# An expert layer on one core: three input buffers, layer norm two batches ahead, probabilities scaled in the transposing matmul

## The chip, the cores and the metric

One core of one Trainium2 chip runs the whole program. The metric is the device time in microseconds (us), the median of a few runs; lower is better. A core has five engines with queues of their own: TensorE (PE), VectorE (DVE), ScalarE (ACT), GpSimd (POOL) and SyncE (SP), which here issues the DMAs.

## What is computed

The reference chains four transformer-like layers over x (16 batches of 256 tokens, 128 wide), with a context of 1601 tokens. The change touches only the second, an expert layer with a cross attention in front. Cut to what matters, in the order of the kernel (weights folded so that the context is used as it comes):

```python
n   = layer_norm(x, eps=1e-5) * gamma + beta          # 256 x 128
q   = n @ Wq
s   = (q @ Wk.T) @ ctx.T / sqrt(128)                  # 256 x 1601
p   = softmax(s)                                      # exp, sum, division by the sum
ev  = (p @ ctx) @ Wv                                  # 256 x 128
f   = concat(n, ev, anchor)                           # anchor: a vector for each batch
r   = softmax(f @ router_W + router_b)                # 3 experts
e_i = gelu_like(f @ e_w1[i] + e_b1[i]) @ e_w2[i] + e_b2[i]
g   = sigmoid(silu(f @ gate_w1 + gate_b1) @ gate_w2 + gate_b2)
out = x + g * ((sum_i r_i * e_i) @ out_w + out_b)
```

All is fp32. The attention layers before and after it are phases of their own.

## The kernel before

`layers` (L1596) runs four parts one after the other, each with its own buffers, semaphores and block: `modulation`, an attention phase (names pa_...), `expert_layer` (L1105, names moe_...), a second attention phase (pb_...). A part starts when the one before it has ended on all engines.

In `expert_layer` a batch has a front F (layer norm, q, transposes of the context, scores, softmax, transposes of the probabilities, pooling of the context, ev) and a back B (router, three experts, gate, output). Steps of the front: ln, xt (xn transposed), q, qk, c0 to c3 (context tiles transposed, four in a step, the last step one), s0 and s1 (scores and softmax of each half of 128 queries), p00 to p03 and p10 to p13 (probabilities of half 0 and 1 transposed, 13 tiles of 128 keys each), pc (26 matmul records: probabilities times context), ev. Steps of the back: r (router), h0, h1, h2 (first expert matmuls), g1, e0, e1 (second expert matmuls and weighting for each half), g2, rt, o.

`walk` (L1214) calls these steps on each engine in one order written out by SCHED. First the whole front of batch 0; then body b runs the back of batch b interleaved with the front of batch b+1, in this order: F ln, B r, F xt, F q, B h0, F qk, F c0, B h1, F c1, F c2, B h2, F c3, F s0, B g1, F s1, F p00, B e0, F p01, F p02, B e1, F p03, F p10, B g2, F p11, F p12, B rt, F p13, F pc, B o, F ev. The last body has only the back. Every engine takes its own share of each step in that order, so a waiting instruction holds up all behind it on its engine.

Who does what: VectorE has ln (L1289 to L1303, 21 instructions, each waiting for the one before it), the copies of c1 and c3, in s0 and s1 the row maxima (L1317), their negation (L1319, L1321), the sum and its reciprocal rec (L1323, L1327), the copies of p01, p03, p11, p13 (`move_probs`, L1241 and L1243), the small router softmax, the products of h and g1 (L1363, L1360), the weighting in e0 and e1 (L1380, L1382). ScalarE has the copies of xt, q, qk, c0, c2, pc, ev, p00, p02, p10, p12, the exp of the scores (L1437) and the tanh of experts and gate. GpSimd has two things: the division of the probabilities by their sum, prn = pr * rec over 128x1601 (L1483), and the final addition xo = y + xin (L1491). TensorE transposes prn in L1549.

Front results go through two PSUM banks in turn: step i of the front writes bank i % 2 and waits until step i-2 is copied out (`bank_free`, L1206). So p02 waits for the copy of p00, p03 for that of p01, and so on.

SP's queue (L1247): `load_x` fetches x, the modulation columns acols and the router row rrow of a batch into one of two buffers each, and waits until the batch two before it is summed (x_sum), because the final addition reads xin; `load_c` fetches the context tile cin (single buffer, 800 KB) and waits for pc of the batch before it; `store` writes xo. Order: load_x(0), load_c(0), load_x(1), load_c(1), store(0), then load_x(k), load_c(k), store(k-1).

Of the kernel before, what the change touches and what calls it, by code (L numbers as in the profile page):

```python
# [17 lines left out]
ALU = mybir.AluOpType  # L18
# [3 lines left out]
P = 128  # L22
B = 16
# [1081 lines left out]
def expert_layer(nc, w, x_src, x_dst, ctx_d, cols_d, rows_d, ident_d, nb):  # L1105
# [20 lines left out]
    with Semaphores(nc) as sems, ExitStack() as ctx:  # L1126
# [17 lines left out]
        xin = [sb(f"xin{i}", [P, QT, D]) for i in range(2)]  # L1144
# [13 lines left out]
        prn = [sb(f"prn{i}", [P, KEYS]) for i in range(QT)]  # L1158
# [15 lines left out]
        x_in, c_in = [sem("x_in0"), sem("x_in1")], sem("c_in")  # L1174
# [17 lines left out]
        X_LOADS = 3 * 16  # L1192
# [21 lines left out]
        def walk(eng, front, back):  # L1214
            def body(b, w, has_next):
                for kind, k in SCHED:
                    if kind == "F" and has_next:
                        front(k, b + 1, 1 - w)
                    elif kind == "B":
                        back(k, b, w)  # L1220
# [26 lines left out]
        def _(sp):  # L1247
# [3 lines left out]
            def load_x(n, w):  # L1251
# [22 lines left out]
            if nb > 2:  # L1274
                for i in range((nb - 2) // 2):
                    for k, w in ((2, 0), (3, 1)):
                        load_x(i * 2 + k, w)
                        load_c(i * 2 + k)
                        store(i * 2 + k - 1)
            store(nb - 1)  # L1280
# [3 lines left out]
        def _(dve):  # L1284
# [4 lines left out]
            def front(k, n, w):  # L1289
                if k == "ln":  # L1290
                    dve.wait_ge(x_in[w], (n - w) * (X_LOADS // 2) + X_LOADS)
                    wait(dve, x_ln, n * QT)
                    link = Chain(dve, ln_dve, n * LN_PER)
                    for t in range(QT):
                        link(dve.bn_stats(st[:, t, :], xin[w][:, t, :]))
# [6 lines left out]
                    for t in range(QT):  # L1302
                        dve.tensor_scalar(xn[:, t, :], xin[w][:, t, :], ag[:, t, 0:1], rs_y[:, t:t + 1], ALU.subtract, ALU.mult).then_inc(x_ln, 1)  # L1303
# [7 lines left out]
                elif k in ("s0", "s1"):  # L1311
# [86 lines left out]
        def _(act):  # L1398
# [5 lines left out]
            def front(k, n, w):  # L1404
# [26 lines left out]
                elif k in ("s0", "s1"):  # L1431
# [3 lines left out]
                    wait(act, s_norm, after(n - 1, QT, qt))  # L1435
# [6 lines left out]
            def back(k, d, w):  # L1442
# [219 lines left out]
```

## Time and profile before

| | |
|---|---|
| time, median of 3 runs | 6419.06 us (6411.44 to 6420.05) |
| profiled execution, own time | 6427.87 us |
| its span | 6426.1 us |
| mean granted TensorE clock | 0.899 |
| PE busy in the span | 5152.7 us (80%) |
| DVE, ACT, POOL busy | 64%, 58%, 27% |
| expert layer in the span | about 2080 to 3042 us |

The profile is of one execution. Times are in us from the start of its span. PE is TensorE's matmuls, PEld its weight loads, which run beside them. "L1549" is a line of the kernel. An entry such as `moe_bank_f<-moe_ident,moe_prn` is output, then inputs, by the program's names, without buffer numbers. `x8` is a count of records; an fp32 matmul is recorded twice, a transpose once. In brackets stands how long the engine had been idle before the first of them, and what ended that. The granted clock is a share of 2.4 GHz: 1.00 is 2.4 GHz, 0.50 is 1.2 GHz.

### The profile page before, as it was taken

What the parts mean: (1) busy time and instruction counts of PE and PEld (TensorE: products, weight loads), DVE (VectorE), ACT (ScalarE), POOL (GpSimd) and SP (SyncE); (2) the same over time, 40 slices, a digit from 0 to 9 for tenths busy, and PEclk for the clock granted to TensorE, in tenths of its full rate; (3) what the DMA queues carried; (4) which work ended last, traced back from release to release, by engine and by line L of the source; (5) the groups of instructions that cost most, each with busy time, mean ns of one, the idle gap of its engine ahead of it and who ended that gap; (6) DMA issues with size and microseconds to landing.
All of it is one profiled execution on the core that took longest, in us unless ns stands there. A gap on an engine that the chain in (4) does not pass through costs nothing.

```text
span 6426.1 us, 123739 instructions
## 1 busy us (share of the span) xinstructions
PE 5152.7 (80%) x48177; PEld 2416.8 (38%) x48177; DVE 4087.9 (64%) x8759; ACT 3696.1 (58%) x5043; POOL 1731.6 (27%) x2614
## 2 busy tenths in 40 slices
PE   3688888888886776776598888888888888888887
PEld 1233333333332555555233333333333333333333
DVE  3476767777763333333577777676777777677674
ACT  1266667676665222222266666666677776666665
POOL 1433343433321111111223232323221322322311
PEclk9699999999988778887589999999999999999998
DMA  1121111111110000000211111111121111111110
GB/s 39 56 57 46 54 40 48 55 45 52 39 41 22 19 14 21 21 16 20 58 38 55 55 47 54 49 49 54 38 66 55 48 47 37 49 49 37 51 39 6
DMA packets 362967, 271.14 MB, mean 42 GB/s; under 512 B 47905, under 2 KB 324991, under 8 KB 362385
## 3 DMA queue, kind: packets, MB, share of 16 engines
q1 hardware_dynamic: 362384, 263.23, 14.4%
q8 instruction: 384, 6.29, 0.4%
q14 instruction: 199, 1.62, 0.1%
HBM read 86.96 MB, written 12.78 MB: 16 GB/s over the span
## 4 chain that ended last, share of the span: by engine, by line
PE 30%; DVE 10%; ACT 6%; issue 4%; POOL 3%; SPq 0%; DMA 0%; ACTq 0%; POOLq 0%
PE pb_obank L896 11%; DVE pb_c_maxs L584 8%; PE pb_dbank L909 6%; PE pb_aunit L871 5%; ACT pb_probs L653 4%; PE pb_aunit L950 2%; PE pb_aunit L943 2%; PE pb_aunit L935 1%; POOL pb_c_cin L770 1%; PE pb_dbank L957 1%; DVE pb_z_maxs L584 1%; PE pb_aunit L983 1%; PE pb_aunit L977 1%; ACT pb_c_srct L686 0%; POOL pb_c_cs_y L766 0%
## 5 line engine op out<-in xcount | busy, mean ns | idle before, releaser
L584 DVE TENSOR_REDUCE pb_c_maxs<-pb_dbank 128x1 f32<-128x512 f32 (+1 forms) x3584 | 2046.7, 627 | 871.1 <-PE pb_dbank L909 862.1
L653 ACT ACTIVATE pb_probs<-pb_aunit 128x1024 f32<-128x1024 f32 (+1 forms) x1792 | 1753.0, 1024 | 598.6 <-PE pb_aunit L871 540.5
L584 DVE TENSOR_REDUCE pa_c_maxs<-pa_dbank 128x1 f32<-128x512 f32 (+1 forms) x1792 | 1025.5, 627 | 470.3 <-PE pa_dbank L909 468.1
L653 ACT ACTIVATE pa_probs<-pa_aunit 128x1024 f32<-128x1024 f32 (+1 forms) x960 | 936.6, 1024 | 296.8 <-PE pa_aunit L871 264.6
L896 PE MATMUL pb_obank<-pb_probs,pb_c_vaug 128*9 128x256 f32 x13312 | 991.3, 398 | 8.5 <-ACT pb_probs L653 7.5
L909 PE MATMUL pb_dbank<-pb_c_kst,pb_c_qst 48*128 48x512 bf16 (+1 forms) x4096 | 854.9, 354 | 115.6 <-DVE pb_c_maxs L584 91.9
L871 PE MATMUL pb_aunit<-pb_c_qst,pb_c_kst 50*128 50x256 bf16 x6144 | 616.6, 284 | 99.2 <-ACT pb_probs L653 55.3
L909 PEld LDWEIGHTS pb_dbank<-pb_c_kst,pb_c_qst 48*128 48x128 bf16 x4096 | 248.1, 95 | 703.7 <-DVE pb_c_maxs L584 454.9
L896 PE MATMUL pa_obank<-pa_probs,pa_c_vaug 128*9 128x256 f32 x6656 | 489.5, 392 | 5.6 <-ACT pa_probs L653 5.3
L909 PE MATMUL pa_dbank<-pa_c_kst,pa_c_qst 48*128 48x512 bf16 (+1 forms) x2048 | 420.4, 354 | 53.4 <-DVE pa_c_maxs L584 46.2
L871 PEld LDWEIGHTS pb_aunit<-pb_c_qst,pb_c_kst 50*128 50x128 bf16 x6144 | 257.9, 97 | 373.4 <-ACT pb_probs L653 121.1
L896 PEld LDWEIGHTS pb_obank<-pb_probs,pb_c_vaug 128*9 128x9 f32 x13312 | 251.3, 91 | 385.2 <-issue 228.9
L871 PE MATMUL pa_aunit<-pa_c_qst,pa_c_kst 50*128 50x256 bf16 x3072 | 303.5, 280 | 56.1 <-ACT pa_probs L653 31.2
L1483 POOL TENSOR_SCALAR moe_prn<-moe_pr,moe_rec 128x1601 f32<-128x1601 f32 x32 | 138.7, 4336 | 558.4 <-DVE moe_rec L1327 558.4
L909 PEld LDWEIGHTS pa_dbank<-pa_c_kst,pa_c_qst 48*128 48x128 bf16 x2048 | 120.6, 95 | 338.4 <-DVE pa_c_maxs L584 203.2
L584 DVE TENSOR_REDUCE pa_z_maxs<-pa_dbank 128x2 f32<-128x512 f32 x256 | 163.6, 684 | 118.8 <-PE pa_dbank L909 118.8
L784 POOL TENSOR_TENSOR pb_c_kf<-pb_c_kf,pb_c_ksp 128x1024 f32<-128x1024 f32 x64 | 114.4, 1787 | 318.0 <-ACT pb_c_ksp L697 318.0
L871 PEld LDWEIGHTS pa_aunit<-pa_c_qst,pa_c_kst 50*128 50x128 bf16 x3072 | 123.4, 96 | 200.4 <-ACT pa_probs L653 68.8
L896 PEld LDWEIGHTS pa_obank<-pa_probs,pa_c_vaug 128*9 128x9 f32 x6656 | 123.5, 90 | 188.4 <-issue 107.7
L1437 ACT ACTIVATE moe_pr<-moe_bank_s,moe_nm 128x400 f32<-128x400 f32 (+1 forms) x128 | 74.4, 594 | 169.2 <-DVE moe_nm L1321 169.2
L584 DVE TENSOR_REDUCE pb_z_maxs<-pb_dbank 128x2 f32<-128x512 f32 x256 | 164.0, 683 | 0.8 <-PE pb_dbank L909 0.8
L751 POOL TENSOR_SCALAR pb_c_rs_v<-pb_c_agg 128x2 f32<-128x2 f32 x32 | 7.9, 246 | 547.2 <-DVE pb_c_agg L598 547.1
(446 smaller groups left out, 7070.9 us busy)
## 6 DMA issues: line engine op xcount, KB each, us to landing
pb_c_kst<-pb_c_ksp SPq DMA_DIRECT2D x384, 200.1 KB
pa_c_kst<-pa_c_ksp SPq DMA_DIRECT2D x192, 200.1 KB
pb_c_cin<-in_ctx SPq DMA_DIRECT2D x32, 768.0 KB
pa_c_cin<-in_ctx SPq DMA_DIRECT2D x16, 768.0 KB
moe_cin<-in_ctx SPq DMA_DIRECT2D x16, 768.0 KB
pb_c_qst<-pb_c_qsp SPq DMA_DIRECT2D x384, 32.0 KB
pa_z_qst<-pa_z_qsp SPq DMA_DIRECT2D x192, 32.0 KB
pa_z_kst<-pa_z_ksp SPq DMA_DIRECT2D x192, 32.0 KB
```

The costliest lines, as they stand in the source:

```text
L584: dve.tensor_reduce(dst, dbank[N % RING_D][:, 0:cnt * width].rearrange("p (s c) -> p s c", s=cnt), AX.X, ALU.max).then_inc(d_free, 1)
L653: act.activation(probs[u % RING_P][0:rows].rearrange("p a i q -> p (a i q)"), src[0:rows, :], ACT.Exp, scale=HD ** -0.5).then_inc(a_free, 1)
L770: pool.tensor_scalar(s.cin[0:rows, t, :], s.cin[0:rows, t, :], s.cs_m[0:rows, t:t + 1], s.cs_y[0:rows, t:t + 1], ALU.add, ALU.mult).then_i ...
L784: pool.tensor_tensor(s.kf[:, part], s.kf[:, part], s.ksp[:, 0, part], ALU.subtract).then_inc(s.k_r, 1)
L871: ins = pe.matmul(dst[:, par * 512 + h * NQ:par * 512 + (h + 1) * NQ], s.kst[b2][lo:lo + K_ROWS + 2, pair, t * P:(t + 1) * P], s.qst[b2][l ...
L896: ins = pe.matmul(obank[32 * h4:32 * h4 + HD + 1, half * NQ:(half + 1) * NQ], s.vaug[i % 2][0:rows, t, 4 * q + h4, :], src, start=(t == 0) ...
L909: ins = pe.matmul(dbank[nd[tok, s.key, i, par] % RING_D][:, col:col + width], s.qst[b2][lo:lo + K_ROWS, p, qt * P:(qt + 1) * P], s.kst[b2] ...
L935: ins = pe.transpose(dst[:, (t - t0) * P:(t - t0) * P + rows], s.cin[0:rows, t, :], ident[0:rows, 0:rows])
L943: ins = pe.matmul(dst[:, at - t0 * P:at - t0 * P + width], w.wkp[:], src[:, at:at + width], start=True, stop=True)
L950: ins = pe.matmul(dst[0:rows, (t - t0) * P:(t - t0 + 1) * P], (s.srct if s.has_ctx else s.xmt)[:, t * P:t * P + rows], w.wv[:], start=True ...
L1437: act.activation(pr[qt][:, at:at + width], sbank[c][:, 0:width], ACT.Exp, bias=nm[:, qt:qt + 1], scale=D ** -0.5, accum_out=sums[:, qt, c: ...
L1483: pool.tensor_scalar(prn[qt][:], pr[qt][:], rec[:, qt:qt + 1], None, ALU.mult).then_inc(s_norm, 1)
```

## The change

- x has three buffers (xin[n % 3]) and a semaphore for each; it is loaded two batches ahead. acols and rrow keep two buffers, have semaphores of their own (cols_in) and are loaded by `load_cols`. r (VectorE) and h0 to g1 (ScalarE) wait for cols_in, ln waits for x alone.
- `walk`: ln leaves its place at the head of the body. ln of batch 1 comes after the front of batch 0; in body b, ln of batch b+2 comes behind entry 15 of the order, that is behind F p00 and ahead of B e0. For VectorE that is behind s1 and ahead of e0, since p00 is not its step.
- GpSimd no longer divides. VectorE makes a diagonal matrix diag = ident * rec (128x128) for each half, at the end of s0 and s1, and TensorE replaces each transpose of a prn tile by an fp32 matmul of the undivided tile pr with diag, which transposes and scales at once.
- ScalarE's exp waits for the last p step of the batch before instead of for the division.
- SP's order: load_x(0), load_c(0), load_x(1), load_cols(0), then for each n: load_x(n+2), load_cols(n+1), load_c(n+1), store(n).

```diff
-        xin = [sb(f"xin{i}", [P, QT, D]) for i in range(2)]
+        xin = [sb(f"xin{i}", [P, QT, D]) for i in range(3)]
...
-        prn = [sb(f"prn{i}", [P, KEYS]) for i in range(QT)]
+        diag = [sb(f"diag{i}", [P, P]) for i in range(QT)]
...
         def walk(eng, front, back):
...
             for kind, k in SCHED:
                 if kind == "F":
                     front(k, 0, 0)
-            body(0, 0, True)
-            if nb > 2:
-                for i in range((nb - 2) // 2):
-                    body(i * 2 + 1, 1, True)
-                    body(i * 2 + 2, 0, True)
-            body(nb - 1, 1, False)
+            front("ln", 1, 1)
+            for b in range(nb):
+                for at, (kind, k) in enumerate(SCHED):
+                    if kind == "F" and k != "ln" and b + 1 < nb:
+                        front(k, b + 1, (b + 1) % 2)
+                    elif kind == "B":
+                        back(k, b, b % 2)
+                    if at == len(SCHED) // 2 and b + 2 < nb:
+                        front("ln", b + 2, b % 2)
...
+            def load_x(n):
+                if n < nb:
+                    wait(sp, x_sum, n - 2)
+                    sp.dma_start(xin[n % 3][:], x_src[n].rearrange("(t p) d -> p t d", p=P)).then_inc(x_in[n % 3], 16)
+
+            def load_cols(n):
+                w = n % 2
                 wait(sp, x_sum, n - 1)
-                sp.dma_start(xin[w][:], x_src[n].rearrange("(t p) d -> p t d", p=P)).then_inc(x_in[w], 16)
-                sp.dma_start(acols[w][:], cols_d[n]).then_inc(x_in[w], 16)
-                sp.dma_start(rrow[w][:], rows_d[n][ROUTER_ROW:ROUTER_ROW + 1, 0:EXPERTS].to_broadcast([P, EXPERTS])).then_inc(x_in[w], 16)
+                sp.dma_start(acols[w][:], cols_d[n]).then_inc(cols_in[w], 16)
+                sp.dma_start(rrow[w][:], rows_d[n][ROUTER_ROW:ROUTER_ROW + 1, 0:EXPERTS].to_broadcast([P, EXPERTS])).then_inc(cols_in[w], 16)
...
-            load_x(0, 0)
+            load_x(0)
             load_c(0)
-            load_x(1, 1)
-            load_c(1)
-            store(0)
...
+            load_x(1)
+            load_cols(0)
+            for n in range(nb):
+                load_x(n + 2)
+                if n + 1 < nb:
+                    load_cols(n + 1)
+                    load_c(n + 1)
+                store(n)
...
-                    wait(dve, s_norm, after(n - 1, QT, qt))
                     dve.reciprocal(rec[:, qt:qt + 1], tot[:, qt:qt + 1]).then_inc(s_rec, 1)
+                    dve.wait_ge(s_rec, after(n, QT, qt))
+                    wait(dve, f_full, after(n - 1, UF, F_AT[f"p{qt}{len(TG) - 1}"]))
+                    dve.tensor_scalar(diag[qt][:], ident[:], rec[:, qt:qt + 1], None, ALU.mult).then_inc(s_norm, 1)
...
-                if k in ("s0", "s1"):
-                    qt = int(k[1])
-                    pool.wait_ge(s_rec, after(n, QT, qt))
-
-                    wait_apart(pool, f_full, after(n - 1, UF, F_AT[f"p{qt}{len(TG) - 1}"]), (ready, 1))
-                    pool.tensor_scalar(prn[qt][:], pr[qt][:], rec[:, qt:qt + 1], None, ALU.mult).then_inc(s_norm, 1)
+                return
...
-                        ins = pe.transpose(dst[0:rows, (t - t0) * P:(t - t0 + 1) * P], prn[qt][:, t * P:t * P + rows], ident[:])
+                        ins = pe.matmul(dst[0:rows, (t - t0) * P:(t - t0 + 1) * P], pr[qt][:, t * P:t * P + rows], diag[qt][:], start=True, stop=True)
```

## Rows read from the trace of the kernel before

**Rows 1.** Busy time by stretch: us, busy us (records), PEclk, DMA share, GB/s.

```profile
2120.08:3011.38 891.30, 645.21 (x2685) 489.43 (x2686) 308.42 (x894) 241.79 (x615) 140.84 (x45) 0.80 0.07 19
```

**Rows 2.** Busy time, one body in four: PE, PEld, DVE, ACT, POOL, clock.

```profile
2475.71:2498.91 23.20, 11.98 (x52) 9.58 (x52) 7.51 (x32) 6.81 (x15) 0.08 (x1) 0.71 0.19 48
2498.91:2506.63 7.72, 6.72 (x20) 3.59 (x20) 3.44 (x9) 3.20 (x10) 0.86 (x1) 1.00 0.01 2
2506.63:2525.23 18.60, 14.35 (x73) 11.54 (x73) 9.40 (x20) 5.35 (x14) 7.80 (x2) 0.82 0.00 0
2525.23:2533.74 8.51, 7.95 (x36) 6.41 (x37) 0.42 (x1) 0.77 (x2) 0.65 (x1) 1.00 0.01 2
```

**Rows 3.** Timeline of that body's start: start us, us, engine, line, op.

```profile
2475.71 0.35 PE L1560 MATMUL moe_bank_g<-moe_rw,moe_nxt 128*128 128x3 f32 x2 [0.57 <-ACT moe_evt L1402]
...
2480.28 0.49 DVE L1295 BATCH_NORM_STATS2 moe_st<-moe_xin 128x6 f32<-128x128 f32 x2 [5.30 <-DMA moe_rrow<-cond_rows]
...
2484.82 0.66 PE L1521 MATMUL moe_bank_f<-moe_ident,moe_xn 128*128 128x128 f32 x2 [8.09 <-DVE moe_xn L1303]
...
2491.32 0.60 PE L1533 MATMUL moe_bank_f<-moe_ident,moe_cin 128*128 128x128 f32 x4
...
2498.91 2.93 PE L1513 MATMUL moe_bank_s<-moe_ct,moe_qk 128*128 128x401 f32 x8 [2.06 <-DVE moe_ct L1310]
```

**Rows 4.** Timeline of TensorE at the start of body 0.

```profile
2120.08 0.39 PE L1560 MATMUL moe_bank_g<-moe_rw,moe_nxt 128*128 128x3 f32 x2 [0.47 <-ACT moe_evt L1402]
...
2121.00 0.42 PE L1521 MATMUL moe_bank_f<-moe_ident,moe_xn 128*128 128x128 f32 x2
2122.57 1.19 PE L1524 MATMUL moe_bank_f<-moe_nxt,moe_wq 128*128 128x256 f32 x2 [1.16 <-ACT moe_nxt L1412]
...
2126.88 0.60 PE L1533 MATMUL moe_bank_f<-moe_ident,moe_cin 128*128 128x128 f32 x4
```

**Rows 5.** Timeline of the next body's start: router matmul and cin's issue.

```profile
2533.74 0.36 PE L1560 MATMUL moe_bank_g<-moe_rw,moe_nxt 128*128 128x3 f32 x2 [0.56 <-ACT moe_evt L1402]
...
2535.78 0.43 SPq L1262 DMA_DIRECT2D moe_cin<-in_ctx  x1
```

**Rows 6.** Busy time by stretch, there: the last two columns are DMA.

```profile
2540.00:2541.00 1.00, 0.00 (x0) 0.00 (x0) 0.83 (x6) 0.00 (x0) 0.00 (x0) 0.50 0.21 48
```

**Rows 7.** Timeline of TensorE in the middle of the body of rows 2.

```profile
2510.25 0.63 PE L1549 MATMUL moe_bank_f<-moe_ident,moe_prn 128*128 128x128 f32 x4 [3.62 <-POOL moe_prn L1483]
...
2511.66 1.22 PE L1574 MATMUL moe_bank_g<-moe_ew,moe_hh 128*128 128x128 f32 x4
...
2519.75 0.71 PE L1574 MATMUL moe_bank_g<-moe_ew,moe_hh 128*128 128x128 f32 x4
...
2520.39 0.48 PE L1575 MATMUL moe_bank_g<-moe_eb,moe_ones 1*128 1x128 f32 x2
...
2522.96 1.09 PE L1549 MATMUL moe_bank_f<-moe_ident,moe_prn 128*128 128x128 f32 x8
```

**Rows 8.** Timeline of VectorE there; the last line is the last body.

```profile
2506.13 3.26 DVE L1360 SCALAR_TENSOR_TENSOR moe_g<-moe_gt,moe_gz 128x256 f32<-128x256 f32 x1 [0.46 <-ACT moe_gt L1457]
...
2509.31 2.00 DVE L1317 TENSOR_REDUCE moe_mx<-moe_bank_s 128x1 f32<-128x401 f32 x4
...
2514.36 0.16 DVE L1327 RECIPROCAL moe_rec<-moe_tot 128x1 f32<-128x1 f32 x1
...
2515.52 0.35 DVE L1380 TENSOR_SCALAR moe_acc<-moe_bank_g,moe_rp 128x128 f32<-128x128 f32 x1 [0.99 <-PE moe_bank_g L1575]
...
2516.56 0.69 DVE L1241 COPY moe_pt<-moe_bank_f 128x512 f32<-128x512 f32 x1
...
3022.26 0.43 DVE L1360 SCALAR_TENSOR_TENSOR moe_g<-moe_gt,moe_gz 128x256 f32<-128x256 f32 x1 [1.05 <-ACT moe_gt L1457]
```

**Rows 9.** Busy time by stretch: a long and a short low stretch of the clock.

```profile
2211.00:2231.50 20.50, 20.03 (x70) 15.96 (x70) 4.50 (x13) 5.35 (x14) 4.34 (x1) 0.51 0.00 1
...
2569.50:2576.50 7.00, 7.00 (x28) 5.77 (x26) 2.13 (x7) 3.50 (x10) 3.93 (x1) 0.51 0.01 2
```

More of the change, by code:

```diff
@@ L1173, in expert_layer @@
         consts, ready, wk_turned = sem("consts"), sem("ready"), sem("wk_turned")
-        x_in, c_in = [sem("x_in0"), sem("x_in1")], sem("c_in")
+        x_in, cols_in, c_in = [sem(f"x_in{i}") for i in range(3)], [sem("cols_in0"), sem("cols_in1")], sem("c_in")
         ln_dve, x_ln = sem("ln_dve"), sem("x_ln")
@@ L1191, in expert_layer @@
             consts_list.append((ew2[:, e], w["e_w2"][e].rearrange("(c p) n -> p c n", p=P), False))
-        X_LOADS = 3 * 16
+        COL_LOADS = 2 * 16
         LN_PER = 2 * QT + RSQRT_LINKS
@@ L1214, in walk @@
         def walk(eng, front, back):
[L1215 to L1220, printed above, removed]
             for kind, k in SCHED:
@@ L1267, in store @@
                 sp.dma_start(x_dst[d].rearrange("(t p) d -> p t d", p=P), xo[:]).then_inc(x_out, 16)
-            load_x(0, 0)
+            load_x(0)
             load_c(0)
-            load_x(1, 1)
-            load_c(1)
-            store(0)
[L1274 to L1280, printed above, removed]
+            load_x(1)
[6 more added lines that the diff above has]
+                store(n)
             sp.wait_ge(x_out, 16 * nb)
@@ L1290, in front @@
                 if k == "ln":
-                    dve.wait_ge(x_in[w], (n - w) * (X_LOADS // 2) + X_LOADS)
+                    dve.wait_ge(x_in[n % 3], (n // 3 + 1) * 16)
                     wait(dve, x_ln, n * QT)
@@ L1294, in front @@
                     for t in range(QT):
-                        link(dve.bn_stats(st[:, t, :], xin[w][:, t, :]))
+                        link(dve.bn_stats(st[:, t, :], xin[n % 3][:, t, :]))
                     link.join_apart((ready, 1))
@@ L1302, in front @@
                     for t in range(QT):
-                        dve.tensor_scalar(xn[:, t, :], xin[w][:, t, :], ag[:, t, 0:1], rs_y[:, t:t + 1], ALU.subtract, ALU.mult).then_inc(x_ln, 1)
+                        dve.tensor_scalar(xn[:, t, :], xin[n % 3][:, t, :], ag[:, t, 0:1], rs_y[:, t:t + 1], ALU.subtract, ALU.mult).then_inc(x_ln, 1)
                 elif k in ("c1", "c3"):
@@ L1336, in back @@
                     link = Chain(dve, r_dve, d * R_PER)
+                    dve.wait_ge(cols_in[w], (d // 2 + 1) * COL_LOADS)
                     wait(dve, b_full, after(d, UB, i))
@@ L1433, in front @@
                     wait(act, s_neg, after(n, QT, qt))
-                    wait(act, s_norm, after(n - 1, QT, qt))
+                    wait(act, f_full, after(n - 1, UF, F_AT[f"p{qt}{len(TG) - 1}"]))
                     for c, (at, width) in enumerate(CH):
@@ L1449, in back @@
                     h = {"h0": 0, "h1": 1, "h2": 2, "g1": 3}[k]
+                    act.wait_ge(cols_in[w], (d // 2 + 1) * COL_LOADS)
                     wait(act, b_full, after(d, UB, i))
@@ L1490, in back @@
                     wait(pool, x_out, 16 * d)
-                    pool.tensor_tensor(xo[:], y[:], xin[w][:], ALU.add).then_inc(x_sum, 1)
+                    pool.tensor_tensor(xo[:], y[:], xin[d % 3][:], ALU.add).then_inc(x_sum, 1)
             walk(pool, front, back)
```

1 line of the change is left out of this document (removed).

## Prediction

> **What bounds the kernel now.** The program is three phases in a row, and the change touches the middle one, the expert layer. I read the stretches by engine first: from the router matmuls of batch 0 to those of batch 15 there are 15 bodies in 891.3 us, 59.4 us each, with a mean granted TensorE clock of 0.80 [rows 1]. The attention phases before and after the layer keep their time; only buffers and order inside the layer change.
>
> Then one body, cut in four [rows 2]: router matmul to first scores (23.2 us, TensorE busy 12.0, clock 0.71), scores (7.7, busy 6.7), second scores to the pooling of the context (18.6, busy 14.4, clock 0.82), pooling to the next router matmul (8.5, busy 8.0). No other engine is near full, so the chain runs through TensorE and its waits. The timeline gives the two large ones. At the body's start TensorE stands 8.09 us until xn is written: x is fetched only when the batch before it is summed, and VectorE then needs 4.4 us of short links for the layer norm (2480.28 to xt's start at 2484.82, less the hop) [rows 3]. In the middle it stands 3.62 us for GpSimd's pass over the probabilities [rows 7]. Behind each the granted clock falls from 2.4 to 1.2 GHz (0.50): the first fall shows in the mean of 0.71 [rows 2], the second lasts 7 us in ten bodies and 20 us in five [rows 9].
>
> **Body start: x loaded and normalised early.** The third buffer lets x of batch n+2 come in while n+1 is worked on, so xn is ready when the router matmul ends. Body 0 of the kernel before already runs like that, since its x was prefetched: router at 2120.08, xt at 2121.00, c0 at 2126.88, that is 6.8 us from router to c0 [rows 4] against 15.6 in a usual body (2475.71 to 2491.32) [rows 3]. What is late next is the context tile cin. Its DMA is still issued about 2.0 us after the router matmul (2533.74 to 2535.78) [rows 5]: on SP's queue the store, x, acols and rrow stand ahead of it in both versions, and the wait on x_sum is the same. The DMA engines are busy with it until about 2540.2 (0.21 of the next microsecond) [rows 6]; with the landing I take router + 6.8 us. TensorE would otherwise be at c0 some 5 us after the router, so up to 1.9 us of a new wait on cin takes the place of the old one. In body 0 cin went out earlier and the clock was low for part of the stretch; both ways end at 6.8. From c0 to the first scores nothing changes: 2498.91 − 2491.32 = 7.6 us, the 2.06 us for ct among them [rows 3]. First stretch: 6.8 + 7.6 = 14.4 instead of 23.2, a gain of 8.8. If cin lands between 6.0 and 7.5 the term moves by −0.8 to +0.7.
>
> **Scores.** Same work, 7.7 us. ScalarE's and VectorE's new waits (p03 or p13 of the batch before, cols_in) are met a whole body early: 0.
>
> **Middle: the division moves into TensorE.** GpSimd's pass of over 4 us goes and p00 needs only diag, a 128x128 tensor_scalar. No row has that exact form; one with a PSUM source takes 0.35 (2515.52) [rows 8], so I take 0.3 and bound it by 0.1 and 0.6. It ends before the second scores do, since the reciprocal of qt 0 comes ahead of g1. So the 3.62 us wait falls to 0.1. A second gain: g1 takes 3.26 us beside GpSimd's pass and 0.43 in the last body, where there is none [rows 8]; the maxima of qt 1 stand behind it, so exp and diag1 come 2.8 us earlier.
>
> Against it, 26 transposes become fp32 matmuls. A transpose is one record, eight of them 1.09 us, 0.11 to 0.14 each; an fp32 matmul is two records: e0's pair (four records) takes 0.71, and 0.64 to the next start, 0.32 for each [rows 7]. I take 0.30 for one with diag, between 0.21 (two records at the transposes' pace) and 0.32: four cost 1.2. The Trainium skill, "Perfetto Trace Analysis", section Transposes, says that a logical transpose should be done as transpose and not as a standard matmul, because it skips the arithmetic. The rows agree on the price (26 × 0.18 = 4.7 us a body); what it doesn't weigh is the GpSimd wait that this buys off.
>
> VectorE also gets ln(n+2) here, 4.4 us, behind s1 and ahead of e0's scaling and of the move of p01. With the end of the second scores (2506.63) as zero: g1 is done by −0.1, maxima to reciprocal as before 5.2 (2509.31 to 2514.5) [rows 8] give 5.1, diag1 5.6, ln 10.0, e0's scaling and the p01 move another 1.7 (2515.52 to 2517.25) [rows 8], so p01's bank is free at 11.8. TensorE: p00 to 1.3; e0, three pairs and three bias matmuls of about 0.4, 3.2, to 4.5; p01 to 5.7 (p00's bank is free by then, ScalarE moves it behind its exps); p02 to 6.9; e1 to 10.1. Then p03 waits on p01's bank until 11.9: a new wait of 1.8 us. After it p03 0.35, p10 1.2, g2 1.65, p11 1.2, p12 1.2, rt 0.3, p13 0.35 and its move 0.4 give 18.6. That is what the stretch takes today: the GpSimd wait and the slow clock are traded for longer matmuls and a wait on VectorE. Bounds: 17.6 (0.21 a matmul) to 19.2 (diag 0.6, matmul 0.32).
>
> **Pooling to router.** 8.5 us, unchanged. The POOL queue keeps only the final addition.
>
> **Sum.** 14.4 + 7.7 + 18.6 + 8.5 = 49.2 us a body with TensorE at the full level wherever it bounds. That is not safe. Body 0 was at the lower level right after its router matmuls although there was no long wait: q's two records of 256 columns take 1.19 us [rows 4], where eight of 400 in the scores take 2.93 [rows 3]. And waits of about 2 us remain at cin, at ct and at p03. A low stretch no longer than the one there, at most the 4.3 us from q to c0, costs up to 2.2 us where it is not hidden behind cin; I take 1.7. I count one: 50.9 a body. Gain: 15 × (59.4 − 50.9) = 127 us, and about 3 us in batch 0's front, which waits twice for GpSimd alone with nothing else to do; the last body has no front and stays. Together 130. The profiled execution took 6427.9 (span 6426.1), 8.8 above the median of the timed runs, 6419.1; I apply the gain to the median: 6289 us.
>
> **Rivals.**
> 1. *All at the full level.* No low stretch is exposed: 49.2 a body, gain 153 + 3, 6263 us. For it: the 3.6 and 8 us waits, after which every long low stretch came, are gone. Against: body 0. Chance 0.22.
> 2. *Long low stretches in a third of the bodies, as now.* Such a stretch over p and e costs the new kernel more than the old: at 0.50 four records take 1.22 instead of 0.71 [rows 7], so a tile costs 0.57, the two e units 11.2, g2 2.9 and the stretch 30.2 instead of 18.6; with 1.5 on the pooling, +13.1. A third of that on 49.2 is 53.6: gain 87 + 3, 6329 us. Chance 0.26.
> 3. *Slower.* The same mechanism in nearly every body: the waits at ct, the second scores and p03 drop the clock and the small matmuls of p and e never bring it back, as in the five stretches of 20 us in which TensorE was busy throughout at 0.50 [rows 9]. It decides from (59.4 − 49.2)/13.1 = 0.78 of the bodies; in all of them a body takes 62.3, 43 us more in all, 3 less for the front: 6459. Against it: ten of fifteen bodies recover after 7 us, even behind a 3.6 us wait. Chance 0.05. The skill's rule on transposes would come true here, as its price is then paid at half speed; that changes none of the numbers.
> 4. *The change doesn't reach the path.* VectorE's or cin's new wait is longer (cin issued behind something I don't see, ln stretched), and most of 8.8 us is given back. It would need 8 us of new waits, no row shows one; some us of it are possible. Chance 0.03 for no difference.
>
> **How the numbers follow.** Forecast 6289 us, chance 0.40; rivals as above; 0.04 for other mixtures, faster by less. A measurement of this kernel tells about 0.2% (13 us) from no change. Faster 0.92, same 0.03, slower 0.05. The range takes in rival 1 with the cheap matmul and most of an earlier cin (48.1 a body, 6247) and rival 2 with a little more (6345).
>
> **What would show it right or wrong.** Right: bodies of 49 to 52 us; xt directly behind the router matmuls; c0 waiting 1 to 2 us for cin; L1483's work gone and p00 starting at once behind the second scores; g1 at 0.43 everywhere; 26 tiles as 52 records a body; p03 waiting 1 to 2.5 us for VectorE's move of p01; granted clock of the layer above 0.9. Wrong: matmuls with diag above 0.35 us at the full level, c0 before router + 6 or behind + 8, low stretches of 20 us in more than a third of the bodies, or attention phases that change.

## The result and the profile after

| | before | after |
|---|---|---|
| time, median of 4 runs | 6419.56 us (6411.44 to 6421.23) | 6321.17 us (6318.98 to 6323.86) |
| profiled execution, own time | 6427.87 us | 6322.98 us |
| its span | 6426.1 us | 6321.2 us |
| router of batch 0 to router of batch 15 | 891.3 us, 59.4 a body | 780.2 us, 52.0 a body |
| granted clock there | 0.80 | 0.87 |

The ratio is 0.9849 with a 95% interval of 0.9832 to 0.9866: 98 us faster, where 130 was forecast (6289 us; the range of 6247 to 6345 holds it). In the two profiles the fifteen bodies give 111.1 us back and everything outside them costs 6.2 us more (6426.1 − 891.3 against 6321.2 − 780.2): 4.3 in the attention phase ahead of the layer and 0.5 in the one behind it, whose code is the same, and 2.5 in the last body, which does the same work at a lower clock (0.64 against 0.72), less 1.1 in batch 0's front.

The stretches of after, first all bodies, then one body in the four parts of [rows 2]. Columns: us, busy us (records) of PE, PEld, DVE, ACT and POOL, granted clock, DMA share, GB/s.

```profile
2123.32:2903.52 780.20, 660.63 (x3076) 512.83 (x3076) 272.49 (x924) 240.67 (x615) 10.78 (x15) 0.87 0.08 21
...
2446.51:2462.03 15.52, 11.88 (x51) 9.52 (x52) 3.79 (x11) 6.70 (x15) 0.07 (x1) 0.78 0.27 72
2462.03:2469.59 7.56, 6.56 (x20) 3.78 (x21) 3.55 (x10) 3.20 (x10) 0.00 (x0) 1.00 0.00 0
2469.59:2489.91 20.32, 17.56 (x100) 14.74 (x98) 10.62 (x42) 5.36 (x14) 0.00 (x0) 0.83 0.00 1
2489.91:2498.42 8.51, 7.95 (x36) 6.41 (x37) 0.43 (x1) 0.77 (x2) 0.65 (x1) 1.00 0.00 0
```

GpSimd is down from 140.8 us [rows 1] to 10.8 and VectorE from 308 to 272. TensorE works 15 us more than before. The body's start is 7.7 us shorter than in [rows 2] (15.52 against 23.20), the middle 1.7 us longer (20.32 against 18.60), though its wait for GpSimd is gone.

The start of that body in the timeline (start us, us, engine, line, op; in brackets the idle time before it and what ended it), to be held against [rows 3]:

```profile
2446.51 0.35 PE L1557 MATMUL moe_bank_g<-moe_rw,moe_nxt 128*128 128x3 f32 x2 [0.57 <-ACT moe_evt L1403]
...
2447.40 0.42 PE L1518 MATMUL moe_bank_f<-moe_ident,moe_xn 128*128 128x128 f32 x2
...
2448.55 0.43 SPq L1262 DMA_DIRECT2D moe_cin<-in_ctx  x1
...
2449.03 1.19 PE L1521 MATMUL moe_bank_f<-moe_nxt,moe_wq 128*128 128x256 f32 x2 [1.21 <-ACT moe_nxt L1413]
...
2454.28 0.71 PE L1530 MATMUL moe_bank_f<-moe_ident,moe_cin 128*128 128x128 f32 x4
...
2462.03 2.93 PE L1510 MATMUL moe_bank_s<-moe_ct,moe_qk 128*128 128x401 f32 x8 [2.06 <-DVE moe_ct L1308]
```

xt follows the router at once: the 8.09 us are gone. But c0 comes 7.77 us behind the router, with no wait for cin. Between lies q at 1.19 us, the lower level; by stretches of 1 us the clock is at 0.50 from about 2448 to 2454. The low stretch isn't tied to the wait before q. In the next body it begins at once, between the second and the third router matmul (0.36 us, then 0.57 for the same form), where TensorE had last waited 0.57 us:

```profile
2498.42 0.35 PE L1557 MATMUL moe_bank_g<-moe_rw,moe_nxt 128*128 128x3 f32 x2 [0.57 <-ACT moe_evt L1403]
2498.64 0.36 PE L1557 MATMUL moe_bank_g<-moe_rw,moe_evt 128*128 128x3 f32 x2
2498.86 0.57 PE L1557 MATMUL moe_bank_g<-moe_rw,moe_nxt 128*128 128x3 f32 x2
```

In ten of the fifteen bodies the clock falls 0.3 to 1.2 us behind the start of the router matmuls, ahead of the wait before q; in four it falls within that wait, in body 0 behind it.

The middle, TensorE, and the low stretch in it:

```profile
2469.59 1.05 PE L1546 MATMUL moe_bank_f<-moe_diag,moe_pr 128*128 128x128 f32 x8
...
2474.98 1.16 PE L1546 MATMUL moe_bank_f<-moe_diag,moe_pr 128*128 128x128 f32 x8 [0.27 <-ACT moe_pt L1403]
...
2481.12 1.79 PE L1546 MATMUL moe_bank_f<-moe_diag,moe_pr 128*65 128x128 f32 x10 [2.01 <-DVE moe_pt L1237]
...
2485.43 3.57 PE L1546 MATMUL moe_bank_f<-moe_diag,moe_pr 128*128 128x128 f32 x16
```

```profile
2481.90:2488.50 6.60, 6.60 (x27) 5.70 (x27) 1.37 (x4) 0.98 (x2) 0.00 (x0) 0.50 0.00 0
```

VectorE at the same time:

```profile
2468.83 0.29 DVE L1327 TENSOR_SCALAR moe_diag<-moe_ident,moe_rec 128x128 f32<-128x128 f32 x1
...
2469.25 0.43 DVE L1361 SCALAR_TENSOR_TENSOR moe_g<-moe_gt,moe_gz 128x256 f32<-128x256 f32 x1
...
2474.86 0.29 DVE L1327 TENSOR_SCALAR moe_diag<-moe_ident,moe_rec 128x128 f32<-128x128 f32 x1
2475.06 0.48 DVE L1293 BATCH_NORM_STATS2 moe_st<-moe_xin 128x6 f32<-128x128 f32 x2
...
2480.38 0.68 DVE L1237 COPY moe_pt<-moe_bank_f 128x512 f32<-128x512 f32 x1
```

p00 starts at once, p03 waits 2.01 us for VectorE's move of p01, which stands behind diag, the layer norm and e0's weighting. From 0.8 us behind the end of that wait the clock is at 0.50 for 6.6 us, in which TensorE is busy throughout; the sixteen records of p11 and p12 take 3.57 us there and 2.05 at the full level (below). All fourteen bodies with a layer norm have the wait of 2.0 us and a low stretch that begins around its end (0.6 us before it to 1.4 us behind it); the fifteenth has neither and takes 46.57 us.

### The profile page after: what moved, and what is told of

Read it like the earlier page. It is cut to its first block, busy times and chain, and to the rows that moved or that the text cites. A ratio compares the mean times of both kernels' runs of the same rounds, so it can differ in the third digit from the quotient of the medians.

```text
span 6321.2 us, 124543 instructions
## 1 busy us (share of the span) xinstructions
PE 5183.3 (82%) x48593; PEld 2450.4 (39%) x48593; DVE 4051.0 (64%) x8791; ACT 3695.1 (58%) x5043; POOL 1592.8 (25%) x2582
## 4 chain that ended last, share of the span: by engine, by line
PE 30%; DVE 10%; ACT 6%; issue 4%; POOL 3%; SPq 0%; DMA 0%; ACTq 0%; POOLq 0%
PE pb_obank L896 11%; DVE pb_c_maxs L584 8%; PE pb_dbank L909 6%; PE pb_aunit L871 5%; ACT pb_probs L653 5%; PE pb_aunit L950 2%; PE pb_aunit L943 2%; PE pb_aunit L935 1%; POOL pb_c_cin L770 1%; DVE pb_z_maxs L584 1%; PE pb_dbank L957 1%; PE pb_aunit L983 1%; PE pb_aunit L977 1%; ACT pb_c_srct L686 0%; POOL pb_c_cs_y L766 0%
## 5 line engine op out<-in xcount | busy, mean ns | idle before, releaser
L1546 PE MATMUL moe_bank_f<-moe_diag,moe_pr 128*128 128x128 f32 (+1 forms) x832 | 139.5, 325 | 35.5 <-DVE moe_pt L1237 28.3
```

The costliest lines, as they stand in the source:

```text
L1546: ins = pe.matmul(dst[0:rows, (t - t0) * P:(t - t0 + 1) * P], pr[qt][:, t * P:t * P + rows], diag[qt][:], start=True, stop=True)
```

## The experiments

All bodies were cut at the same five points of TensorE's timeline (starts of router, c0, first scores, p00, pc, next router), means of fifteen bodies in us. "Outside" is the span less the fifteen bodies. Each row is one profiled execution, which can lie anywhere among its kernel's times: e1's (6425.82 us) and e5's (6288.96) are the longest of theirs, e3's (6249.77) is the shortest.

| kernel | router to c0 | to s0 | to p00 | to pc | to router | body | outside |
|---|---|---|---|---|---|---|---|
| before | 14.97 | 7.65 | 11.44 | 16.59 | 8.78 | 59.42 | 5534.8 |
| after | 7.91 | 7.70 | 8.28 | 19.55 | 8.58 | 52.01 | 5541.0 |
| e1 x ahead alone | 7.78 | 7.79 | 12.64 | 20.72 | 9.31 | 58.23 | 5550.5 |
| e2 diagonal alone | 14.99 | 7.65 | 7.75 | 15.12 | 8.51 | 54.02 | 5518.7 |
| e3 after, ln behind p13 | 7.83 | 7.78 | 8.50 | 15.13 | 8.51 | 47.74 | 5531.6 |
| e4 after, transposes | 7.90 | 7.88 | 8.30 | 18.15 | 9.80 | 52.04 | 5527.7 |
| e5 = e4 with e3's order | 7.73 | 7.68 | 8.68 | 15.45 | 9.05 | 48.59 | 5558.4 |
| e6 = e1 with e3's order | 7.65 | 7.66 | 12.68 | 17.76 | 9.11 | 54.86 | 5549.5 |
| e7 after, p03's wait filled | 7.89 | 7.67 | 8.43 | 17.08 | 8.51 | 49.57 | 5543.8 |
| e8 = e3, the start's waits filled | 8.41 | 7.87 | 7.56 | 15.12 | 8.51 | 47.47 | 5547.8 |
| e9 = e6, p00's wait filled | 7.67 | 7.77 | 12.13 | 13.70 | 8.91 | 50.19 | 5528.6 |
| e10 = e3, two cin buffers | 7.21 | 7.69 | 7.84 | 15.12 | 8.51 | 46.37 | 5526.0 |
| e11 = e3 again | 7.87 | 7.86 | 8.69 | 15.13 | 8.51 | 48.07 | 5525.9 |

**One part at a time: e1 and e2.** e1 is after with `prn`, GpSimd's division and the transposes restored:

```diff
-                        ins = pe.matmul(dst[0:rows, (t - t0) * P:(t - t0 + 1) * P], pr[qt][:, t * P:t * P + rows], diag[qt][:], start=True, stop=True)
+                        ins = pe.transpose(dst[0:rows, (t - t0) * P:(t - t0 + 1) * P], prn[qt][:, t * P:t * P + rows], ident[:])
```

> The changed kernel with only its first part: three x buffers, ln two batches ahead at the same place in the body; GpSimd divides again and the probabilities are transposed as before. My theory: the whole gain is the body start (router to c0 7.9 instead of 15.0 us in the mean of 15 bodies, 7 us a body), and the diagonal matrix is worth about nothing. In the middle the kernel before moved p01 at 10 to 10.6 us behind the second scores with TensorE arriving at p03 at 14.2; with ln's 4.4 us in front of it VectorE moves p01 at about 14.2, so ln is hidden by the GpSimd wait. So 59.4 - 7.1 = 52.3 us a body, time 6320 us, as the changed kernel (6305 to 6345). Rival A (the diagonal matrix carries a third or more of the gain): 6355 us or more. Rival B (the low clock behind the remaining GpSimd wait gets worse, long stretches in most bodies): above 6370.

Measured: 6398.75 us, ratio 0.9978 (0.9956 to 1.0001): next to nothing. TensorE in the middle of a body:

```profile
2409.37 0.63 PE L1549 MATMUL moe_bank_f<-moe_ident,moe_prn 128*128 128x128 f32 x4 [3.62 <-POOL moe_prn L1483]
...
2412.81 1.22 PE L1574 MATMUL moe_bank_g<-moe_ew,moe_hh 128*128 128x128 f32 x4
...
2414.69 1.97 PE L1549 MATMUL moe_bank_f<-moe_ident,moe_prn 128*128 128x128 f32 x8
...
2423.21 1.12 PE L1549 MATMUL moe_bank_f<-moe_ident,moe_prn 128*65 128x128 f32 x4 [3.18 <-DVE moe_pt L1237]
```

TensorE's waits over all bodies (waiting line, what ended it: us in total, times, longest):

```profile
PE moe_bank_f L1549 <- POOL moe_prn L1483: 54.3, 15, 3.6
...
PE moe_bank_f L1549 <- DVE moe_pt L1237: 26.7, 14, 3.2
```

The start gives 7.2 us a body as it should. The parts behind it take 6.0 back (0.1 to the scores, 1.2 to p00, 4.1 to pc, 0.5 in the pooling): the wait for GpSimd stands as before, a second one on VectorE stands at p03, 3.2 us in this body and 1.9 on the mean, and the clock is low behind them. How much is order and how much clock e6 and e9 tell.

e2 is before with the diagonal alone; x and the layer norm are as they were, GpSimd has the addition left.

> The kernel before with only the second part: diagonal matrix on VectorE, fp32 matmuls in place of the transposes, no division on GpSimd; x loads and ln as before. My theory: the 3.6 us wait is traded for longer matmuls, and without ln in the middle p03 does not wait (the last front of the changed kernel, which has no ln in it, takes 15.1 us from p00 to pc instead of 18.7 to 20.3). A body is 15.0 + 7.7 + 7.6 + 15.1 to 17 + 8.5 = 53.9 to 55.8 us against 59.4: 54 to 82 us faster, 6337 to 6366 us. Rival (the transpose price outweighs: 26 x 0.18 = 4.7 us a body more than the 3.6 us of wait): 16 us slower, 6435 us.

```diff
-                        ins = pe.transpose(dst[0:rows, (t - t0) * P:(t - t0 + 1) * P], prn[qt][:, t * P:t * P + rows], ident[:])
+                        ins = pe.matmul(dst[0:rows, (t - t0) * P:(t - t0 + 1) * P], pr[qt][:, t * P:t * P + rows], diag[qt][:], start=True, stop=True)
```

Measured: 6346.22 us, ratio 0.9892 (0.9865 to 0.9919). The middle takes 15.12 or 15.13 us in every one of the fifteen bodies, so no low stretch is left in it, with the layer norm out of the way.

**The layer norm's place: e3.** One line in `walk`:

```diff
-                    if at == len(SCHED) // 2 and b + 2 < nb:
+                    if k == "p13" and b + 2 < nb:
```

> The changed kernel with ln(n+2) moved on VectorE from behind p00 to behind p13, where VectorE idles 7.5 us during pc. My theory: the wait of p03 for VectorE's copy of p01 (2.02 us in each of 14 bodies) is ln's, so the stretch p00 to pc falls from 19.5 in the mean to the last body's 15.1, or to 16.9 if low stretches of the clock stay: 37 to 62 us faster than the changed kernel, 6259 to 6284 us. Rival (p03's wait is replaced by a wait of xt or of y at the end of the body, or the clock eats it): within 10 us of the changed kernel's 6321.

Measured: 6255.23 us, ratio 0.9755 (0.9730 to 0.9780), some 60 us below after (0.9849 − 0.9755 of 6420). The middle of one body:

```profile
2432.24 1.16 PE L1546 MATMUL moe_bank_f<-moe_diag,moe_pr 128*128 128x128 f32 x8 [0.27 <-ACT moe_pt L1403]
...
2436.30 1.33 PE L1546 MATMUL moe_bank_f<-moe_diag,moe_pr 128*65 128x128 f32 x10
...
2439.03 2.05 PE L1546 MATMUL moe_bank_f<-moe_diag,moe_pr 128*128 128x128 f32 x16
...
2441.98 1.75 PE L1536 MATMUL moe_bank_f<-moe_pt,moe_cin 128*128 128x256 f32 x7 [0.47 <-DVE moe_pt L1239]
```

No wait at p03 and 15.12 or 15.13 us in all fifteen bodies instead of 19.55 on the mean: 4.4 us a body. The layer norm at the end of the body delays nothing: xt still follows the router at once.

**How much of that is the wait, how much the clock: e7.** After's order, with four matmuls that nobody reads ahead of p03, in a bank of the scores that is free by then:

```diff
+            def fill(n, count):
+                wait(pe, s_exp, after(n, QT * NCH, QT * NCH - 1))
+                for _ in range(count):
+                    pe.matmul(sbank[3][:, 0:NQ], ident[:], gw1[:].rearrange("p c n -> p (c n)"), start=True, stop=True)
...
+                if k == "p03" and 0 < n < nb - 1:
+                    fill(n, 4)
```

> The changed kernel with four dummy fp32 matmuls of 256 columns (1.7 us at the full clock) into a free scores bank ahead of p03, in the 14 bodies in which VectorE has ln there: TensorE works instead of standing 2.02 us; nothing else moves. It parts the wait from the clock behind it. Theory (the idle time brings the low stretches of 7 to 10 us that follow p03): p00 to pc falls from 19.5 in the mean to 17.1 (15.1 and the wait), 34 us faster than the changed kernel, 6287 us. Rival (the clock doesn't follow the idle time there, or the dummies delay p03): 6321 or more.

Measured: 6285.93 us, ratio 0.9786 (0.9768 to 0.9805).

```profile
2500.64 1.99 PE L1502 MATMUL moe_bank_s<-moe_gw,moe_ident 128*128 128x256 f32 x8
2502.74 1.33 PE L1553 MATMUL moe_bank_f<-moe_diag,moe_pr 128*65 128x128 f32 x10
...
2505.47 2.05 PE L1553 MATMUL moe_bank_f<-moe_diag,moe_pr 128*128 128x128 f32 x16
```

p03 starts 11.5 us behind p00 as in after, since VectorE's move is as late, but TensorE isn't idle before it. The middle is 17.21 to 17.23 us in all fourteen bodies with a layer norm, at the full level throughout. In those fourteen after takes 19.87 us on the mean ((15 × 19.55 − 15.12) / 14) and e3 15.13. So the layer norm's place costs after 4.7 us a body: 2.1 are the wait itself (17.22 against 15.13), 2.65 the low clock behind it.

**Is the fp32 matmul the dearer one? e4 and e5.** After, and e3, with plain transposes of the undivided probabilities:

```diff
-                        ins = pe.matmul(dst[0:rows, (t - t0) * P:(t - t0 + 1) * P], pr[qt][:, t * P:t * P + rows], diag[qt][:], start=True, stop=True)
+                        ins = pe.transpose(dst[0:rows, (t - t0) * P:(t - t0 + 1) * P], pr[qt][:, t * P:t * P + rows], ident[:])
```

> The changed kernel with the 26 matmuls with diag turned back into transposes, of the undivided probabilities; diag is still made and waited for. The division by the sum is left out. It prices matmul against transpose. My theory: 0.15 us a tile (1.16 us for four matmuls, 0.55 for four transposes), but the tiles ahead of p03 (12) only lengthen its wait for VectorE, so 14 tiles count: 2.1 us a body, 32 us, 6289 us. Rival A (all 26 count, or a better clock adds to it): 6262 us or below. Rival B (TensorE's activity falls with the transposes and the clock drops more often): 6321 or above.

> The changed kernel with ln(n+2) behind p13 and with plain transposes of the undivided probabilities; the division by the sum is left out. Against the kernel that only moves ln (6255 us, 15.13 us from p00 to pc in every body) it prices the 26 matmuls where nothing else waits. Theory (arithmetic price): the last body of the run with transposes and ln in the middle took 13.37 us from p00 to pc at the full clock, so 1.75 us a body, 26 us less, 6229 us. Rival (transposes bring more low clock with them, as in the run with ln in the middle, where p00 to pc took 18.5 us with either): no gain or a loss, 6255 to 6290 us.

Measured: e4 6316.33 us, ratio 0.9850 (0.9825 to 0.9875), the same as after; e5 6274.92 us, ratio 0.9771 (0.9747 to 0.9795), the same as e3 within the intervals. The cheaper operation bought nothing. In e4 p03 starts 11.54 us behind p00, as in after, in the eleven bodies that show a wait for VectorE there, only the wait is 2.5 us instead of 2.0; of the 1.4 us that are saved up to pc the pooling behind it takes 1.2 back (9.80 against 8.58), at the lower clock. Two bodies of e5 show the other half, one at the full level and one with a low stretch:

```profile
2541.27 0.66 PE L1546 MATMUL moe_bank_f<-moe_ident,moe_pr 128*128 128x128 f32 x4 [1.22 <-ACT moe_pt L1403]
...
2546.99 1.09 PE L1546 MATMUL moe_bank_f<-moe_ident,moe_pr 128*128 128x128 f32 x8
```

```profile
2489.43 1.12 PE L1546 MATMUL moe_bank_f<-moe_ident,moe_pr 128*128 128x128 f32 x4 [1.22 <-ACT moe_pt L1403]
...
2499.65 1.97 PE L1546 MATMUL moe_bank_f<-moe_ident,moe_pr 128*128 128x128 f32 x8
```

With transposes p02 comes before ScalarE has moved p00, and a wait of 1.22 us appears where the matmuls leave 0.27. Nine bodies pass it and take 13.36 us from p00 to pc; six fall to the lower level around its end and take 18.4 to 18.7. Whether the shorter wait or the kind of work keeps e3 up isn't told apart by these two runs.

**Why x ahead alone brought nothing: e6 and e9.** e6 is e1 with the layer norm behind p13 (the line of e3).

> Three x buffers and ln two batches ahead, but placed behind p13; GpSimd divides, transposes as before. It asks where the gain of the x-ahead part (7.2 us at the body start) went when it was alone (only 16 us faster in all). Theory 1 (ln in front of p01's copy ate it): with ln out of the way the middle is that of the kernel before (11.4 + 16.6 + 8.8 us in the mean), a body 52.3 us, 6308 us. Theory 2 (the low clock behind the GpSimd wait ate it, ln has little part in it): long low stretches stay, p00 to pc 19.5 or more, 6350 to 6400 us.

Measured: 6376.90 us, ratio 0.9936 (0.9917 to 0.9955). The wait at p03 is gone, the one for GpSimd is there, and behind it stands the low clock again:

```profile
2535.71 0.63 PE L1549 MATMUL moe_bank_f<-moe_ident,moe_prn 128*128 128x128 f32 x4 [3.61 <-POOL moe_prn L1483]
...
2541.35 1.97 PE L1549 MATMUL moe_bank_f<-moe_ident,moe_prn 128*128 128x128 f32 x8
```

Nine of its bodies take 19.0 to 20.1 us from p00 to pc, six take 15.0 to 15.2. So neither theory holds alone: moving the layer norm gives 3.4 us a body (58.23 to 54.86), not 5.9, and low stretches stay, though not in all bodies. e9 fills that wait and leaves its cause in place:

```diff
+                    if k == "p00" and n:
+                        for _ in range(8):
+                            pe.matmul(dst[:, 0:NQ], ident[:], gw1[:].rearrange("p c n -> p (c n)"), start=True, stop=True)
                     wait(pe, s_norm, after(n, QT, qt))
```

> Kernel e6 (x ahead, GpSimd divides, transposes, layer norm of batch b+2 behind p13) with eight extra matmuls ahead of p00, written to p00's own bank and overwritten by it, 0.43 us each at 2.4 GHz, so about 3.4 of the 3.6 us that TensorE stands there for GpSimd. The wait itself stays; only the standing idle goes. Theory (the idle of that wait brings the low clock that costs e6 its gain): no low stretch behind p00, p00 to pc 15.0 us as in e6's undisturbed bodies instead of 17.8, and 0.3 us less behind pc; scores to p00 as before 12.7. A body of about 51.8 instead of 54.86, and 15 x 3 = 46 us less: 6331 us (6320 to 6345). Rival (the low clock there has another cause, such as the earlier wait of 1 us on ScalarE or the small matmuls of e): p00 to pc stays at 17 to 18 us and the time at 6370 to 6385, or above if the extra matmuls run on past the wait.

Measured: 6290.69 us, ratio 0.9801 (0.9774 to 0.9829), 40 us below what I expected:

```profile
2396.00 3.62 PE L1548 MATMUL moe_bank_f<-moe_gw,moe_ident 128*128 128x256 f32 x16
2399.69 0.66 PE L1552 MATMUL moe_bank_f<-moe_ident,moe_prn 128*128 128x128 f32 x4
...
2410.67 1.09 PE L1552 MATMUL moe_bank_f<-moe_ident,moe_prn 128*128 128x128 f32 x8
```

All bodies, first of e6, then of e9:

```profile
2121.26:2944.18 822.92, 672.46 (x2686) 503.54 (x2686) 308.84 (x894) 240.75 (x615) 140.73 (x45) 0.81 0.08 20
```

```profile
2122.40:2875.25 752.85, 647.39 (x2926) 487.55 (x2926) 307.64 (x894) 240.72 (x615) 140.82 (x45) 0.91 0.08 22
```

The same work, the same waits on GpSimd (its 140.8 us are untouched) and 240 records more: 70 us less, and the clock 0.91 instead of 0.81. From p00 to pc 13.24 or 13.25 us in the seven bodies at the full level, where I had taken the 15.0 of e6's better bodies for undisturbed; those hold a low stretch of 7 us too, and that is the miss. The other eight (13.7 to 15.5) still have one of 3 to 7 us late in the middle, 9 to 11 us behind p00, where TensorE had last waited 0.54 us; no run tells what brings it. With GpSimd still dividing, this kernel is below after.

**The low stretches at the body's start: e8 and e10.** e8 is e3 with such extra matmuls ahead of q (two), c0 (three) and the first scores (four).

```diff
+                if k in ("q", "c0") and n:
+                    fill(n - 1, 2 if k == "q" else 3)
...
+                if k == "s0" and n:
+                    fill(n - 1, 4)
```

> The kernel with ln behind p13 and dummy matmuls in the three other waits: two ahead of q, three ahead of c0, four ahead of the first scores, 3.9 us of work at the full clock in waits of 1.2, about 1.6 and 2.06 us. Theory: the remaining low stretches lie behind these waits (router to c0 7.83 us where cin would allow 6.7; s0 to p00 8.5 instead of 7.56), so a body falls from 47.7 to 45.5 us: 34 us faster, 6221 us. Rival (the low clock there comes from the small router matmuls, or the dummies lie on the path): 6255 us or more.

Measured: 6254.81 us, ratio 0.9741 (0.9722 to 0.9759), no better than e3's 0.9755 within the intervals. The low stretch behind the wait for ct is gone: scores to p00 takes 7.56 us in all bodies, 0.94 less than in e3. But router to c0 grows by 0.58 (8.41 against 7.83). In ten bodies a low stretch stays there (2458.50 to 2465.50 in one: TensorE busy 6.99 of 7.00 us at 0.51). In seven of them it begins ahead of the first extra matmul, so filling the wait before q can't prevent it; the extra matmuls run at the lower level too, and q starts up to 3.9 us behind the router instead of 2.5. In the other five the clock stays up as far as c0's wait, and c0 waits 0.80 to 2.76 us for cin instead (7.4 to 9.4 us behind the router). Its body takes 47.47 us.

e10 is e3 with cin in two buffers, fetched a body early; e11 is e3 again on the same chip.

```diff
+            load_c(1)
             for n in range(nb):
                 load_x(n + 2)
                 if n + 1 < nb:
                     load_cols(n + 1)
-                    load_c(n + 1)
                 store(n)
+                load_c(n + 2)
```

> Kernel e3 with a second buffer for the context tile cin, fetched a whole body early: nothing on TensorE waits for cin. Theory A (where cin waits it hides a start of the body that runs at the low clock anyway, as in after, where only 4 of 15 bodies wait for cin): router to c0 goes from 7.8 to between 7.0 and 7.5 us, 5 to 12 us less in all, 6243 to 6250 us. Theory B (cin bounds the start; without it the start runs at the full level): router to c0 near 6.0 us, 15 x 1.8 = 27 us less, 6228 us. Theory C: nothing (within 6250 to 6260), because the stretch is set by the chain xt, q, qk and its copies.

> Kernel e3 once more, on the chip of the two others, as the measure for the one with two cin buffers: 6255 us (6249 to 6262), and a body again of 47.6 to 47.9 us with no low stretch between p00 and pc.

Measured: e10 6224.24 us (6216.76 to 6233.54), ratio 0.9699 (0.9671 to 0.9726); e11 6248.26 us (6240.39 to 6252.04), ratio 0.9733 (0.9701 to 0.9765). A body of e11 in which c0 waits for cin, then one of e10:

```profile
2457.60 0.63 PE L1530 MATMUL moe_bank_f<-moe_ident,moe_cin 128*128 128x128 f32 x4 [1.02 <-DMA moe_cin<-in_ctx]
...
2465.26 4.62 PE L1510 MATMUL moe_bank_s<-moe_ct,moe_qk 128*128 128x401 f32 x8 [2.06 <-DVE moe_ct L1308]
```

```profile
2355.22 0.64 PE L1534 MATMUL moe_bank_f<-moe_ident,moe_cin 128*128 128x128 f32 x4
...
2362.89 2.93 PE L1514 MATMUL moe_bank_s<-moe_ct,moe_qk 128*128 128x401 f32 x8 [2.06 <-DVE moe_ct L1312]
```

The time is theory B's (6228), the way there isn't. Router to c0 is 7.21 us (7.77 or 6.69 in turn), which is theory A's; the rest comes from the scores: the wait for ct is 2.06 us in both, but scores at the lower level (9.0 to 10.3 us instead of 7.56) follow it in ten bodies of e11 and in two of e10. In five of those ten c0 had waited for cin (0.33 to 2.15 us), in the other five no such wait shows, so the wait for cin isn't the whole cause; the changed order of the transfers may have its part. That is open. e10 is the best of all kernels here: 194 us below before, nearly twice what the change brings.

## Why the prediction was right, and where its sum was off

1. *x early, right.* xt directly behind the router, 8.09 us gone. The term router to c0 was 6.8 and is 7.91. It was read from body 0 of before [rows 4], and after's own body 0 has 6.89. The others have 7.6 to 9.2 (four beyond + 8, which was named as a sign of being wrong). In most it is the low stretch that begins at the router matmuls and lasts until c0 (c0 7.77 behind the router without any wait for cin). The prediction had seen it in body 0 and took it for no longer than the 4.3 us from q to c0; it begins ahead of the wait before q in ten bodies and is about 7 us long in twelve. e8 fills that wait and leaves a low stretch in ten bodies.
2. *The new wait on cin, half right.* cin is issued 2.04 us behind the router, as forecast. But c0 waits for it visibly in four bodies of fifteen (0.73 to 1.33 us); in the rest TensorE at half speed is itself too late. Hiding the one behind the other was allowed for, not that it would be the usual case. e10: without the wait on cin router to c0 falls by 0.66 us only.
3. *The division in TensorE, right in kind, too dear.* diag takes 0.29 us (taken 0.3), g1 0.43 everywhere, p00 starts at once. A tile costs 0.26 (sixteen records in 2.05 us), not 0.30, against 0.14 for a transpose (eight in 1.09). That is 3.1 us for 26 tiles, not 4.7, and from p00 to pc only 1.76 are left of it (15.12 in e3 against 13.36 in e5), of the difference 0.95 because the transposes wait that much longer for ScalarE's move at p02. At the lower level a tile costs 0.45 (3.57 for eight), where rival 2 took 0.57. At the full level the middle is 17.22 us (e7), 1.4 under the forecast 18.6.
4. *The new wait on VectorE, right.* 2.02 us in fourteen bodies, forecast 1.8; the layer norm ends at +9.8 us from p00 (10.0), the bank is free at +11.5 (11.8).
5. *The low clock, the term that failed.* I counted one exposed low stretch of 1.7 us a body. The shortest values that the runs show for each part of the same work (6.7 in e10, 7.64 and 7.56, 17.08 on the mean in e7, 8.51) make 47.5 us, so a body of 52.0 holds 4.5 us of low clock, and at the start of four bodies of the wait for cin with it: 1.2 at the start (e10's 6.7 itself has a low stretch of about 3.5 us, so this is a lower bound), 0.1 up to the scores, 0.7 in them, 2.5 from p00 to pc and 0.1 in the pooling. I had named the waits at ct and p03 but counted one low stretch only, of the length of the one at q. The sum of 50.9 was near because two errors went against each other: 49.2 for the full level was 1.7 too high, 1.7 for the clock 2.8 too low; that they nearly cancel is luck. The sign "clock of the layer above 0.9" failed with it: 0.87. Of the 32 us between the forecast gain of 130 and the measured 98, 16 lie in the bodies; 9 lie outside them (6.2 more where 3 less were forecast); the rest, 6.5, is that before's profiled execution was 8.3 us above its median and after's 1.8.
6. *Batch 0's front*: forecast 3 us, measured 1.1 (53.17 to 52.08 us from the layer's first work to its first router).
7. *Rivals.* The all-full-level one (6263) didn't come; e7 and e3 show what it needs, no idle time at p03. The one with long low stretches in a third of the bodies gave 6329, near the measured time, but by another mechanism: after has no stretch of 20 us there, it has one of 3 to 10 us in all fourteen bodies with a layer norm. The slower case was far off. Nearest to that fear is e1 (clock 0.50 to 0.62 from p00 to pc in all fifteen bodies, and still not slower than before), where waits of 3.6 and up to 3.2 us follow each other.

By the medians x ahead alone brings 16 us (an interval that holds no change), the diagonal alone 69, both 98, both with the layer norm behind p13 160. 16 and 69 make 85; the 13 us to 98 are no more than the intervals allow, so in time the two parts add within the noise. But x ahead gives only 1.2 us a body of the 7.2 that it saves at the start. Each part leaves idle time on TensorE that the other's place makes costly: x ahead shortens the start, and the layer norm's new place and the low clock behind GpSimd's wait take it back (e1; e6 moves the layer norm, 3.4 us a body; e9 fills the wait, another 4.7); the diagonal removes that wait, and the layer norm's new place puts one of 2.0 us in (e7).

Of the Trainium skill, "Perfetto Trace Analysis", section Transposes (transposes skip the arithmetic and are to be preferred to a standard matmul), the runs show this: at the full level it holds in price, 13.36 against 15.12 us for the 26 tiles and what lies between. In the time of the kernel it doesn't: e4 is level with after and e5 with e3, since the transposes bring a longer wait and, in six bodies of e5, the lower clock.

## What to carry to other kernels

A wait on the chain of a TensorE-bound loop can cost more than its length: here the one of 2.0 us at p03 cost 2.1 us in itself and 2.65 in the clock behind it. It need not: scores at the lower level follow the wait of 2.06 us for ct in ten bodies of e11 and in two of e10. So put a price on both cases and look at the granted clock in the microseconds around each wait of the profile. To know which part is the clock, fill the wait with matmuls that nobody reads and see that the step behind it starts no later: in e7 p03 still starts 11.53 us behind p00. Where the low stretch begins ahead of the wait, this buys nothing (e8). And when a step is moved off the head of the chain, look for the place where nothing of its engine's later work is waited for; a few entries' distance (behind p13 instead of behind p00) was worth some 60 us, more than half as much again as the whole change brought.

## What was unexpected of the hardware

- Sixteen records of fp32 matmul with no use, 3.62 us a body, made a kernel 86 us faster by the medians of e6 and e9 (ratios 0.9936 and 0.9801, on two chips), 70 of them in the bodies.
- TensorE stays at the lower level while it is busy without a gap: 6.60 of 6.60 us in after, 20.03 of 20.50 in before [rows 9]. Low stretches around the end of p03's wait in after were about 3.5 us long in five bodies, 7 in seven and 10 in two; behind GpSimd's wait in before they were 7 in ten and 20 in five.
- Low stretches also began where TensorE had waited no longer than 0.57 us (router matmuls in after) or 0.54 (late in the middle of e9). What brings those is open.
- Eight tiles in a row take 2.05 us as fp32 matmuls at the full level and 3.57 at the lower one, and 1.09 and 1.97 us as transposes: a transpose at the lower level costs as much as the matmul at the full one.
- Code that is the same but for batch 0's front took different times in different profiles: outside the fifteen bodies 5518.7 us (e2) to 5558.4 (e5), 0.6% of the whole. A gain inside one phase is read better from its own bodies than from one run's total.
